# Ternary gated layer and embedding products written out tile by tile, with the row sum moved behind the tile's maximum

## What is computed

```python
h = jax.nn.silu(jnp.einsum('blk,kd->bld', patches, W1) + b1)
return jnp.einsum('bld,de->ble', h, W2) + b2
```

```python
def _act_quant(x):
    scale = 127.0 / jnp.clip(jnp.max(jnp.abs(x), axis=-1, keepdims=True), 1e-05)
    xq = jnp.clip(jnp.round(x * scale), -128.0, 127.0) / scale
    return x + jax.lax.stop_gradient(xq - x)
...
gate = jax.nn.silu(_bitlinear(x, w_gate))
up = _bitlinear(x, w_up)
return _bitlinear(gate * up, w_down)
```

## Time and profile before

| | us |
|---|---|
| median of 3 runs | 1436.33 |
| their range | 1435.38 to 1437.99 |
| the profiled execution, its own time | 1424.37 |
| its span in the profile | 1422.2 |
| VectorE busy | 1031.1 (73%) |
| TensorE busy | 1034.2 (73%) |

### The profile page before, as it was taken

How to read it: one execution, slowest core, us unless ns; L and a number is a source line. 1 busy time by engine, 2 the same in 40 slices (tenths; PEclk the granted TensorE clock), 3 DMA queues, 4 the chain that set the end, 5 groups by cost and what they waited for, 6 DMA issues and landing times. The chain is left out here.

```text
span 1422.2 us, 28260 instructions
## 1 busy us (share of the span) xinstructions
PE 1034.2 (73%) x9099; PEld 698.1 (49%) x9099; DVE 1031.1 (73%) x2238; ACT 751.4 (53%) x1493; POOL 564.6 (40%) x674
## 2 busy tenths in 40 slices
PE   3548778763399997685756869266479997459996
PEld 2422223223265663463544766144456665448885
DVE  5779999987455655647977865788758886746665
ACT  5557777742375663215435654243348887334442
POOL 0248888862244434721001100000026665335663
PEclk9669999995699999886968979688769999579998
DMA  6001111101265654312000000000023332322231
GB/s 235 16 6 54 38 44 45 37 1 53 82 162 151 171 143 155 91 34 89 1 1 1 1 1 1 1 0 0 0 77 103 109 121 76 105 50 77 78 78 36
DMA packets 50611, 89.66 MB, mean 63 GB/s; under 512 B 10740, under 2 KB 34111, under 8 KB 49635
## 3 DMA queue, kind: packets, MB, share of 16 engines
q1 hardware_dynamic: 41840, 64.19, 14.3%
q0 software_dynamic: 8352, 21.67, 5.9%
q10 hardware_dynamic: 288, 2.10, 0.5%
HBM read 73.04 MB, written 16.05 MB: 63 GB/s over the span
## 5 line engine op out<-in xcount | busy, mean ns | idle before, releaser
L1133 POOL TENSOR_TENSOR scan_ch<-scan_hs,scan_ct 128x452 f32<-128x452 f32 x128 | 143.6, 1144 | 41.1 <-DVE scan_hs L1247 41.0
L1158 PE MATMUL scan_py<-scan_ch,ident 128*128 128x452 f32 x256 | 131.4, 604 | 37.2 <-POOL scan_ch L1133 27.8
L1247 DVE TENSOR_TENSOR_SCAN scan_hs<-scan_abar,scan_bx 128x452 f32<-128x452 f32 x128 | 133.0, 1080 | 1.4 <-DVE scan_bx L1239 0.8
L1158 PEld LDWEIGHTS scan_py<-scan_ch,ident 128*128 128x128 f32 x256 | 41.7, 196 | 105.6 <-POOL scan_ch L1133 98.2
L2275 DVE TENSOR_SCALAR m3x_a<-m3x_ph,m3x_b 128x128 f32<-128x128 f32 x184 | 49.7, 343 | 58.4 <-ACT m3x_ah L2253 58.4
L1207 ACT ACTIVATE scan_abar<-ssm_dt,ssm_a 128x448 f32<-128x448 f32 x128 | 80.0, 634 | 13.8 <-DVE scan_hs L1247 13.2
L2253 ACT ACTIVATE m3x_ah<-m3x_ph,m3x_b 128x128 f16<-128x128 f32 x184 | 49.9, 383 | 70.4 <-PE m3x_ph L463 39.9
L3204 POOL TENSOR_TENSOR mha_prob_lo<-mha_prob,mha_prob_hi 113x452 f16<-113x452 f32 x64 | 65.8, 1051 | 37.7 <-ACT mha_prob_hi L3373 37.7
L461 PE MATMUL m3x_ph<-m3x_xb,m_w_hi 128*128 128x128 f16 x368 | 74.0, 220 | 2.5 <-DVE m3x_al L2286 1.8
L462 PE MATMUL m3x_ph<-m3x_xb,m_w_hi 128*128 128x128 f16 x368 | 74.0, 220 | 0.0
L463 PE MATMUL m3x_ph<-m3x_xb,m_w_lo 128*128 128x128 f16 x368 | 73.8, 220 | 0.0
(11 more groups left out here) (702 smaller groups left out, 3835.7 us busy)
## 6 DMA issues: line engine op xcount, KB each, us to landing
mha_wbuf<-m3w SPq DMA_DIRECT2D x32, 512.0 KB, 3.3
scan_piece<-m0w SPq DMA_DIRECT2D x30, 256.0 KB, 2.7
m0x_b<-m0b SPq DMA_DIRECT2D x57, 128.0 KB, 3.4
m_out<-m0x_yo SPq DMA_DIRECT2D x57, 128.0 KB, 2.3
tok_wbuf<-m0w SPq DMA_DIRECT2D x5, 768.0 KB, 12.0
m3x_b<-m3b SPq DMA_DIRECT2D x23, 128.0 KB
m_rows<-m0r_parts SPq DMA_DIRECT2D x4, 448.0 KB
m_res<-h SPq DMA_DIRECT2D x1, 1792.0 KB, 8.1
```

What stands on the lines that cost most here:

```text
L1133: pool.tensor_tensor(ch[r][:], hs[r][:], ct[n % 2][:], ALU.mult).then_inc(weighed, 1)
L1158: pe.matmul(py[c][:, 0:GT], core.ident[:], ch[u % R][:], start=n == 0, stop=n == NS - 1).then_inc(summed, 1)
L1247: dve.tensor_tensor_scan(hs[u % R][:], abar[c][:, 0:GT], bx[u % R][:], 0.0, ALU.mult, ALU.add).then_inc(scanned, 1)
```

## The change

The three loops of the gated layer and the one of the embedding products become straight-line code with fixed addresses and fixed semaphore values. In VectorE's step of a tile the sum into the rows, `add(at + -2)`, now stands behind the maximum instead of ahead of it. The maximum signals a new semaphore, `reduced`, and the first small step waits for that after the sum has been issued; the chain has four steps a tile in place of five.

```diff
-                with pe.Fori(0, NB // 2) as i:
-                    for j in range(2):
-
-                        pe.wait_ge(emb_free[j], i)
-                        tok = bass.ds(i * (2 * LP) + j * LP, LP)
-                        for k in range(KC):
-                            last = mm3(pe, emb[j][0:LP, :], g_hi[:, k, tok], g_lo[:, k, tok],
-                                       w2_hi[:, k, :], w2_lo[:, k, :], k == 0, k == KC - 1)
-                        last.then_inc(emb_ready[j], 1)
+                for b in range(NB):
+                    j = b % 2
+
+                    need(pe, emb_free[j], b // 2)
+                    tok = slice(b * LP, (b + 1) * LP)
+                    for k in range(KC):
+                        last = mm3(pe, emb[j][0:LP, :], g_hi[:, k, tok], g_lo[:, k, tok],
+                                   w2_hi[:, k, :], w2_lo[:, k, :], k == 0, k == KC - 1)
+                    last.then_inc(emb_ready[j], 1)
...
-                    with pe.Fori(0, NB // 2 - 1) as i:
-                        for u in range(2):
-                            step(At(i, 1 + u, 2))
+                    for j in range(1, NB - 1):
+                        step(At(0, j, 2))
...
+                        dve.wait_ge(gu_done, j * 2 + 2)
+                        dve.tensor_reduce(out=amax[p][:], in_=gu[p][:], op=ALU.max, axis=AX.X,
+                                          apply_absolute_value=True).then_inc(reduced, 1)
                         if behind:
                             add(at + -2)
-                        dve.wait_ge(gu_done, j * 2 + 2)
-                        ch = Chain(dve, chain_sem, j * 5)
-                        ch.step(dve.tensor_reduce(out=amax[p][:], in_=gu[p][:], op=ALU.max, axis=AX.X,
-                                                  apply_absolute_value=True))
+                        dve.wait_ge(reduced, j + 1)
+                        ch = Chain(dve, chain_sem, j * 4)
                         ch.step(dve.tensor_scalar(amax[p][:], amax[p][:], 1e-5, None, ALU.max))
...
-                    with dve.Fori(0, NB // 2 - 1) as i:
-                        for u in range(2):
-                            step(At(i, 2 + u, 2), True)
+                    for j in range(2, NB):
+                        step(At(0, j, 2), True)
```

More of the change, by code:

```diff
@@ L3013, in stage_bit_glu @@
             g_ready, silu_done, gu_done = st.sem("g_ready"), st.sem("silu_done"), st.sem("gu_done")
-            chain_sem, quant = st.sem("chain"), st.sem("quant")
+            chain_sem, quant, reduced = st.sem("chain"), st.sem("quant"), st.sem("reduced")
             t_ready, copied, o_ready, o_free = ([st.sem(f"{n}{p}") for p in two] for n in (
@@ L3087, in _ @@
                     gate(At(0, 0, 2))
-                    with act.Fori(0, NB // 2 - 1) as i:
-                        for u in range(2):
-                            gate(At(i, 1 + u, 2))
-                            copy_turned(At(i, u, 2))
+                    for j in range(NB - 2):
+                        gate(At(0, j + 1, 2))
+                        copy_turned(At(0, j, 2))
                     gate(At(0, NB - 1, 2))
```

## The result

The changed kernel took 1416.88 us, the median of 4 executions (1416.49 to 1423.54); the kernel before, run beside it, took 1435.86 (1432.51 to 1437.99). The ratio is 0.9884 with a 95% interval of 0.9857 to 0.991, which is 13 to 20.5 us less.

A forecast was written before the change was run, and what follows sets the result against it. No single engine bounds the kernel; in the gated layer, VectorE's work plus its wait for TensorE's down product sets the tile time. Savings of 9.6 + 1.3 = 10.9 us gave 1436.3 - 10.9 = 1425.4 us, range 1421.5 to 1430.0.

The forecast's parts named there:

- The gated layer, 9.6 us forecast: Gated layer: the maximum covers VectorE's wait for the down product in 14 tiles, saving 9.6 us.
- the two bounds: Gated layer's saving: 9.3 us if stretches at 1.2 GHz stay, 9.9 us if there are none.
- the low stretches: Gated layer: TensorE at 1.2 GHz, lengthening the sum's wait to 1.07 to 1.55 us in four of 14 tiles.
- TensorE late: Gated layer: VectorE waits for the silu, 1.6 us a tile in one to three tiles; 1428.0 us, chance 0.18.
- The clock stays up: Gated layer and embedding: no low clock between, last down products faster too; saving 13.0 us, 1423.3 us, chance 0.11.
- Given back later: Attention stage: weight loads fixed in time swallow 9.6 us, leaving 1.3 or less; 1435.0 us, chance 0.08.
- Slower: Gated layer: TensorE's clock stays low, all 14 tiles take 6.68 us; 11.6 us slower, 1448 us, chance 0.03.
- The loops of the gated layer, zero: Gated layer: writing out its loops gives zero, bounded by 0.3 us on either side.
- The embedding, 1.3 us: Embedding products: removing the loop's pauses saves 1.2 us and an earlier start 0.1, together 1.3 us.
- The estimate of 0.9 us for the loop: Embedding products: the skill page's branch times put the loop's cost at 0.9 us, so 0.4 us less saved.
- The sum, 10.9 us: Whole kernel: 9.6 us from the gated layer plus 1.3 us from the embedding products, 10.9 us saved.

The follow-up runs named there:

- e1: The kernel before, unedited, timed beside itself: 1436.34 us, ratio 1.0003.
- e5: The changed kernel again, unedited, against the kernel before: 1422.55 us, ratio 0.9910.
- e12: The changed kernel a third time, unedited, against the kernel before: 1423.81 us, ratio 0.9920.
- e6: The kernel before with the sum moved and the embedding products written out, the gated layer's loops kept: 1420.56 us, ratio 0.9916.
- e7: The kernel before with the sum moved and the gated layer's loops written out, the embedding loop kept: 1424.20 us, ratio 0.9921.
- e3: The kernel before with only the sum moved behind the maximum, all loops kept: 1425.71 us, ratio 0.9939.
- e10: The changed kernel with 12 of the 48 row gathers (output differs), against the kernel before: 1411.28 us, ratio 0.9840.
- e4: The kernel before with only the gated layer's three loops written out, old order and embedding loop kept: 1434.67 us, ratio 1.0001.
- e2: The kernel before with only the embedding products written out: 1433.75 us, ratio 0.9986.
- second and third comparison: Two repeats of the unedited changed kernel against the kernel before: 1422.55 and 1423.81 us, ratios 0.9910 and 0.9920.

## Why the prediction was wrong, and what of it was right

**The gated layer, 9.6 us forecast: right.** The profile shows 9.9, and 10.1 to 10.2 between e1 and e5 or e12. Each step is there: the maximum 1.44 us behind the halves (1.43 forecast), the overlap of 0.08, the first small step at 2.97, a tile of 5.06 (5.07), 0.2 us of wait in the one low tile that still waits. The rule of the Trainium skill's page VectorE: DVE Perf Modes (section "The DRAIN you can't avoid") that was weighed, by which an instruction waits until the one before has drained and the layer would save 1.0 us less, is not borne out by the row: the sum starts at 953.92 while the maximum runs to 954.00. The prediction left out that the same section adds that a next instruction "that is not held starts earlier", and the row agrees with that. Of the two bounds, 9.3 with the low stretches and 9.9 without, the upper one was reached, but not because the low stretches went: e6 and e7 have more of them (clock 0.85) and save 9.6 against e1. They now fall on the gate and up products and no longer on most of the down product that a sum waits for. That the move alone does it is shown by e3.

**TensorE late: it came in three profiles, at a thirtieth of its price.** In the changed kernel's first profile ScalarE's silu ends nobody's wait, with 0.1 us to spare where the products before it were slow. In e6, e7 and e10 it holds VectorE's second half in every second tile, for 0.05 us. The prediction's 1.6 us a tile was mis-read: the tile of 6.68 us is 1.17 longer than one of 5.51 because its sum waits 1.55 us in place of 0.37, and that is the wait that the move covers. **The clock stays up: fell.** It asks for 11.7 us in the layer, 1.8 of them at the last two down products; their sums wait 2.74 and 0.96 us, where it was 2.75 and 1.22, and against e1 the layer saves 9.6 to 10.7. That its 1423.3 us lies nearer to the second and third medians than the forecast does is chance. **Given back later: fell**, since the executions are shorter by at least as much as the layer and the token stage are. **Slower: fell**, and a clock of 0.85 did not make it come. (The middle that is given for TensorE late, 1428.0, should by its own savings of 9.3 and 6.1 be 1428.6.)

**The loops of the gated layer, zero: right in the whole, wrong alone.** The prediction compared steps of VectorE inside and outside the loop, and found them alike, because "its register rows hide under the work before". None of the steps compared stands behind a wait. The sum does, and there e4 shows 0.14 us a tile.

**The embedding, 1.3 us: right.** The token stage is 1.6 us shorter in the first pair of profiles, and 1.4, 1.5 and 2.2 between e1 and e2, e5 and e12. The intervals are 0.67, not the 0.65 assumed, so the loop's pauses were 1.0 us over the 12 intervals and not 1.2; counted from the stage's first multiply the start came 0.28 us earlier, as forecast. The rest differs from one execution to the next with the moment at which the multiplies become fast: the stage takes 28.8 to 30.2 us in the seven profiles with the embedding written out and 30.4 to 31.2 in the seven without, 1.3 us apart in the mean. (The estimate of 0.9 us for the loop would take 0.3 us off the saving and not the 0.4 given.)

**The sum, 10.9 us: right in all comparisons but the first.** The parts multiply to 0.9986 x 0.9939 x 1.0001 = 0.9926, 10.6 us. The pair with few gathers gives 9.6 to 11.0, the second and third comparison 12.9 and 11.5, with intervals that hold 10.9. The first, of four executions, gave 13 to 20.5 us and does not.

**The step that failed** is the one between the sum and the range: "The timed runs are 12 us longer than it; nothing in the profile says why, and I take the saving as the same there: 1436.3 - 10.9 = 1425.4", and then a range that "takes in the forecast and most of the two beside it". That the saving is the same agrees with the second and third comparison. But the 12 us were the sign of something that the range left out: executions of one program differ, by 11 us in 30 of the kernel before (1430.37 to 1441.33), and in the changed one by the same (1415.33 to 1427.59 over the 16 of the three comparisons). Of the first four of these, three fell at 1416.5 to 1417.1 and made the median; of the twelve others one is under 1419. The three medians, 1416.88, 1422.55 and 1423.81, are 7 us apart for the same kernel. The range was 8.5 us wide and built from the change's costs alone; even the 2.9 us that the prediction takes as what a measurement can tell from no change is not in it. A median of a few executions needs a term of its own, here at least half the distance of those three medians, 3.5 us; and even so widened to 1418.0 the range would have missed the first by 1.1. That the first comparison was a low draw is the reading that the runs favour and is not shown: four drawn at random from the sixteen have a median as low in 49 of 1820 cases, and nothing here tells a low draw from something of that occasion.

**What stays open.** The mean of the changed kernel's 16 executions is 1421.6 us. Against some 1435, which the kernel before gives on every occasion, that is 13.4 us, where the gated layer and the token stage explain 11.6 to 12.4 (e1 against e5 and e12). The stage of the first experts is 162.1 to 163.7 us in five of the seven profiles with the embedding written out and 164.0 to 165.4 in the seven without, but 165.3 and 167.7 in the other two of the changed kernel; the attention stage is either 174.8 to 175.0 or 176.4 to 178.0, with no order in which kernel shows which. Whether the missing 1 to 2 us lie there or are chance the runs do not settle. Nor do they settle what holds the two engines in the shared expert's stage: the ends of matrix multiplies are modelled, so that TensorE itself may have been held while its rows look done. That fewer gathers remove it and save 11 to 14 us is shown. That the code's place in memory decides it was a theory for the differing stages; it fell, because e1, e4 and e7 show the stall with everything ahead of it unmoved, and one program shows it (e1) and does not (its first profile).

## What to carry to other kernels

When an in-order engine waits for a product in front of work that does not need it, put that work ahead of the wait: here a maximum of 1.2 us covered 0.37 us of wait at full clock and over 1 us at low clock, and it did so whether the granted clock was 0.85 or 0.97. A loop's register and address rows cost something behind a wait and nothing behind work, so judge them at the waiting instruction and not at its neighbours. And before trusting two profiles or four timings, run the unchanged kernel a dozen times: if the profiled execution lies outside the timed ones, compare stages between two profiles of the same program before giving a range.

## What the runs showed of the hardware

- In the shared expert's stage ScalarE and VectorE stood for 4 to 27 us at a time, in most cases with "remote" as releaser, while GpSimd issued 36 gathers with hardly a pause, or up to 9 us behind them. Every profile with all 48 gathers but the first of before shows such waits, in a stage of 100 to 107 us that takes 89 to 92 without. I had not looked at this stage, since the change does not touch it.
- Cutting these gathers from 48 to 12 took 0.8% and 0.9% off the kernel, as much as the change itself.
- One list of instructions of the gated layer ran at a granted clock of 0.95 to 0.97 in three executions (changed, e5, e12) and of 0.85 in a fourth (e10), with the gate and up products slow in every second tile and idle times ahead of the transposes of 1.93 and 0.20 us by turns instead of 1.88 each time. The layer took 89.0 to 89.1 us in the first and 89.6 in the last. What decides between the two no run shows.
- The overlap of independent neighbours on VectorE, 0.08 us, is the same with the maximum ahead of the sum (1.14 us from start to start for a maximum of 1.22) as with the sum ahead of the maximum in the earlier trace rows, and the semaphore `reduced`, on which the next step waits, adds nothing to it.
